# First expert stage of a two-layer kernel: four token buffers, expert numbers read ahead, the output bias added by VectorE, and the next layer's first row begun inside the stage

## The chip, the cores and the metric

The kernel is one program on one core of a Trainium2 chip. The metric is the device time of one launch in microseconds (us). One execution of the kernel before was also profiled, with every engine's instructions recorded; its span runs from the first recorded instruction to the last.

## The reference, cut to what matters

Two layers, each of which adds to a residual the product of an attention and a gated mixture of experts, over 8 rows of 512 tokens with 128 channels:

```python
x = L0_attn_x                                   # (8, 512, 128), float32
xn = _layernorm(x)
s = _L0_attn_ref(xn, ...)                       # 16 heads, top-8 sparse attention, memory keys
g = _silu(_L0_ffn_ref(xn, ...))                 # 8 experts, top 2
x = x + s * g
xn = _layernorm(x)
s = _L1_attn_ref(xn, ...)                       # attention over channels
g = _silu(_L1_ffn_ref(xn, ...))                 # 8 experts, top 2, limited capacity
x = x + s * g
```

The change is in the first mixture of experts, which for each token and each of its two experts `e` computes

```python
h1 = X @ W1[e] + b1[e];  h3 = X @ W3[e] + b3[e]      # 128 -> 256 each
h = silu(h1 * h3)
y = h @ W2[e] + b2[e]                                # 256 -> 128
```

and mixes the two results with the gate's weights. The last product with `Wf` is folded into `W2` and `b2` beforehand.

## The kernel before, in words

The five engines run their own programs and meet only at semaphores. Layer 0's attention is done row by row (`row(b)` on every engine): row 0, then the expert stage for all tokens, then rows 1 to 7; layer 1 follows. While row 0 runs, GpSimd scatters the normalised tokens in DRAM (`x0_slots`) into tiles of 128 that each belong to one expert; `tile_e` holds the expert's number of each of the 72 tiles. The expert stage then takes 18 groups (q) of 4 tiles, in 36 duos (d) of 2 tiles, so that q = d // 2. One duo goes through this chain:

- SyncE loads a group of tokens into one of two buffers `xg0[q % 2]`; TensorE turns it into the bank `tr` (`turned0`); ScalarE and VectorE split it into a high and a low part (`high0`, `low0`), again two buffers.
- TensorE: `up0(d)`, 6 matmuls of 512 columns, the weights chosen by a register that holds the expert's number.
- VectorE: `hidden0(d)`, two adds of the expert's bias out of the banks, also chosen by number. GpSimd: the product of the two halves, into `hu0`. ScalarE: `tanh0`. VectorE: `silu0`, into `hh0`.
- TensorE: `hh_turned0(d)` into the bank `sa`; ScalarE: `turned0(d)` copies it out; TensorE: `down0(d)`, into one of the two banks `mbs[q % 2]`.
- When a group's two duos are done, ScalarE copies the bank to `y0_sb[q % 2]` (`y0_out`), GpSimd adds the output bias of each tile's expert in four adds (`y0_bias`), and SyncE stores the group to `y0_slots` (`store_y0`).

On TensorE the order is written out by hand: iteration d does `up0(d)`, at even d `turned0(d // 2 + 1)`, then `hh_turned0(d - 2)` and `down0(d - 3)`. An expert's number is read from `tile_e` by `value_load`, an instruction of the engine's sequencer, directly ahead of the instruction that uses it, once per tile on TensorE (line 1799), VectorE (line 1365) and GpSimd (line 698). SyncE's queue is in order too: the load of group q, then the store of group q - 4, then, early on, a load of 256 KB of `x` for later.

After the stage TensorE waits for the last `y0_out`, turns row 1's tokens (`x_turned(1)`), ScalarE and VectorE split them (`x_highs`, `x_lows`), and row 1 begins with `keys(1, 0, 0)`, three matmuls from `mt_hl`, which GpSimd splits (`split_m`) after its last `y0_bias`. `scores` needs those keys copied out by ScalarE and VectorE and a piece from GpSimd (`next_g`).

Of the kernel before, what the change touches and what calls it, by code (L numbers as in the profile page):

```python
# [30 lines left out]
P = 128  # L31
# [45 lines left out]
def build(nc, x, Wq, Wk, Wv, pre, post, mem_k, mem_v, Wo, bo, W1, b1, W3, b3, W2, b2, Wg, bg, Wf, bf,  # L77
          norm_w, norm_b, qkv_w, qkv_b, proj_w, proj_b, Wr, V1, c1, V2, c2, out, x0_slots, y0_slots, x_slots, y_slots):
    with ExitStack() as ctx:
# [148 lines left out]
        xg0 = [y0_pick[:, i, :, :] for i in range(2)]  # L228
# [92 lines left out]
        xg0_loaded = [sem("xg0_loaded0"), sem("xg0_loaded1")]  # L321
# [11 lines left out]
        y0_copied = sem("y0_copied")  # L333
# [165 lines left out]
        def _(sp):  # L499
# [65 lines left out]
            for q in range(GROUPS0):  # L565
                if q >= 2:
                    sp.wait_ge(xg0_turned, q - 1)
                sp.dma_start(xg0[q % 2], x0_slots[q * T:(q + 1) * T].rearrange("(s p) c -> p s c", p=P)
                             ).then_inc(xg0_loaded[q % 2], 16)
                if q >= 4:  # L570
                    store_y0(q - 4)
                if q == 2:
                    sp.wait_ge(su_pe, SU_BIASES)
                    sp.wait_ge(raw_read, 1)
                if 2 <= q < B + 2:
                    sp.dma_start(x1_all[:, q - 2, :].rearrange("p (t c) -> p t c", c=C),
                                 x[q - 2].rearrange("(t p) c -> p t c", p=P)).then_inc(x1_in, 16)
            for q in range(GROUPS0 - 4, GROUPS0):
                store_y0(q)
# [59 lines left out]
        def _(pool):  # L639
# [54 lines left out]

            def y0_bias(q):
                pool.wait_ge(y0_copied, q + 1)
                for j in range(NT):
                    e = pool.value_load(tile_e[0:1, NT * q + j:NT * q + j + 1], min_val=0, max_val=E0 - 1)
                    y = y0_sb[q % 2][:, j * C:(j + 1) * C]
                    ins = pool.tensor_tensor(y, y, b2f_b[:, bass.ds(e, 1), :].rearrange("p o c -> p (o c)"), ALU.add)  # L700
                ins.then_inc(y0_ready, 1)
# [172 lines left out]
            for d in range(DUOS0):  # L874
# [44 lines left out]
        def _(act):  # L919
# [80 lines left out]

            def y0_out(q):
                act.wait_ge(y0_ps, 2 * q + 2)
                if q >= 2:
                    act.wait_ge(y0_stored[q % 2], 16 * (q // 2))
# [208 lines left out]
        def _(dve):  # L1213
# [987 lines left out]
```

## Time and profile before

| | us |
|---|---|
| median of 3 runs | 1522.11 |
| lowest and highest | 1516.35, 1522.14 |
| the profiled execution's time | 1525.78 |
| its span | 1524.0 |
| TensorE busy | 1395.9 (92%) |
| VectorE busy | 1102.7 (72%) |
| GpSimd busy | 888.6 (58%) |
| ScalarE busy | 809.9 (53%) |

The profile calls TensorE PE (its weight loads PEld), VectorE DVE, ScalarE ACT, GpSimd POOL and SyncE SP; a q behind the name is the engine's sequencer or queue. Buffer numbers are left out of names (`y_pick` is `y0_pick`, `x_slots` also `x0_slots`, `h` is `h1`, `sc` the five score banks). Busy time is a share of the whole span, over stages with different limits. The expert stage lies between about 243 and 389 us. The profiled execution took 1.8 us more than its span.

### The profile page before, as it was taken

The page shows a single profiled execution, that of the slowest core. Times are in us where ns is not written, and L with a number is a line of the kernel's source. Part 1 is how long each engine was busy: PE and PEld are TensorE (multiplying, and loading weights), DVE is VectorE, ACT ScalarE, POOL GpSimd, SP SyncE. Part 2 cuts the span into 40 slices and gives each one's busy share as a digit, 9 for nine tenths or more (in the row PEclk, how much of TensorE's full clock was granted, in tenths as well). Part 3 has the DMA queues.
Part 4 walks back from the last instruction along what each step waited for, and adds up shares of the span by engine and source line. Part 5 has one row for each costly group of instructions (what it writes and reads, how often), then busy time and mean ns, then how long its engine had stood idle before and what let it go on. Part 6 is the DMA issues. An engine that isn't in the chain of part 4 may idle for free.

```text
span 1524.0 us, 32740 instructions
## 1 busy us (share of the span) xinstructions
PE 1395.9 (92%) x10049; PEld 1201.6 (79%) x10049; DVE 1102.7 (72%) x3639; ACT 809.9 (53%) x1737; POOL 888.6 (58%) x1766
## 2 busy tenths in 40 slices
PE   5999998888799899999999999999999999899964
PEld 5558887777688789888988988898898889788842
DVE  7727775566587678878878887887887778654765
ACT  4546663444455556656665656666566566532321
POOL 5247773667666745655574565557456576723552
PEclk9999999999899999999999999999999999999997
DMA  7025001322500000000000000000000000012221
GB/s 242 15 94 187 22 23 54 105 77 64 159 15 9 17 11 9 8 13 16 8 17 12 9 10 12 15 9 17 12 10 7 6 24 9 10 43 69 75 78 41
DMA packets 70108, 62.27 MB, mean 41 GB/s; under 512 B 10808, under 2 KB 58019, under 8 KB 69938
## 3 DMA queue, kind: packets, MB, share of 16 engines
q1 hardware_dynamic: 61746, 44.96, 9.8%
q0 software_dynamic: 8192, 15.23, 3.4%
q8 instruction: 84, 1.38, 0.4%
q14 instruction: 86, 0.70, 0.2%
HBM read 32.88 MB, written 25.17 MB: 38 GB/s over the span
## 4 chain that ended last, share of the span: by engine, by line
PE 63%; DVE 13%; issue 8%; POOL 7%; ACT 3%; POOLq 2%; DMA 2%; DVEq 1%; SPq 0%; ACTq 0%
PE sa L1863 15%; PE sc L1841 11%; PE mb L1870 11%; PE tr L1852 7%; PE sc L1707 4%; DVE kept L1401 3%; DVE top L1391 3%; POOL attn L797 2%; PE mb L2077 2%; PE sc L1843 2%; PE sc L1802 2%; POOL x_slots L766 1%; PE sa L1907 1%; PE tr L1712 1%; PE sc L2065 1%
## 5 line engine op out<-in xcount | busy, mean ns | idle before, releaser
L797 POOL TENSOR_SCALAR attn<-kept,rden 128x128 f32<-128x128 f32 (+3 forms) x512 | 286.4, 559 | 368.5 <-DVE rden L1405 314.4
L1863 PE MATMUL sa<-wv,attnT 128*128 128x128 f32 x2560 | 383.5, 281 | 16.3 <-ACT wv L1010 15.2
L1391 DVE MAX8 top<-sc 128x8 f32<-128x144 f32 (+3 forms) x512 | 263.2, 514 | 174.0 <-PE sc L1843 172.1
L1841 PE MATMUL sc<-k_hl,x_hl 128*128 128x272 f32 (+3 forms) x1920 | 374.2, 315 | 3.1 <-issue 3.1
L1034 ACT ACTIVATE attnT<-tr 128x128 f32<-128x128 f32 (+3 forms) x512 | 223.7, 437 | 267.5 <-PE tr L1852 257.3
L1863 PEld LDWEIGHTS sa<-wv,attnT 128*128 128x128 f32 x2560 | 327.8, 193 | 44.7 <-ACT wv L1010 44.5
L1028 ACT ACTIVATE ex<-sc,nmax 128x144 f32<-128x144 f32 (+3 forms) x512 | 276.6, 540 | 94.3 <-DVE nmax L1393 86.2
L1841 PEld LDWEIGHTS sc<-k_hl,x_hl 128*128 128x128 f32 x1920 | 284.8, 192 | 22.7 <-issue 12.3
L1401 DVE SCALAR_TENSOR_TENSOR kept<-sc,top,ex 128x144 f32<-128x144 f32 (+3 forms) x512 | 289.4, 565 | 1.1 <-issue 1.1
L1852 PE MATMUL tr<-ident,attn 128*128 128x128 f32 x1280 | 230.0, 278 | 25.6 <-POOL attn L797 23.3
L1852 PEld LDWEIGHTS tr<-ident,attn 128*128 128x128 f32 x1280 | 139.6, 143 | 34.9 <-POOL attn L797 31.8
L802 POOL TENSOR_SCALAR attn_mem<-kept,rden 128x16 f32<-128x16 f32 x512 | 144.2, 282 | 0.0
L1870 PE MATMUL mb<-n_all,xnT 128*128 128x128 f32 x1024 | 142.1, 282 | 0.0
L1870 PEld LDWEIGHTS mb<-n_all,xnT 128*128 128x128 f32 x1024 | 126.2, 194 | 0.0
L1843 PE MATMUL sc<-causal,ident_h 128*128 128x128 bf16 x512 | 118.7, 232 | 0.0
L1870 PE MATMUL mb<-x_hl,w_hl 128*128 128x512 f32 x336 | 108.9, 433 | 5.1 <-POOL w_hl L710 3.7
L1010 ACT ACTIVATE k_hl<-mb 128x512 fp32r<-128x512 f32 x128 | 76.5, 597 | 62.9 <-PE mb L1870 62.7
L1383 DVE TENSOR_TENSOR k_hl<-mb,k_hl 128x512 fp32r<-128x512 f32 x128 | 88.5, 692 | 12.0 <-ACT k_hl L1010 11.3
L1405 DVE RECIPROCAL rden<-den 128x1 f32<-128x1 f32 x512 | 83.9, 164 | 17.8
L691 POOL DMA_INDIRECT x_slots<-arena,take x64 | 66.7, 1042 | 43.6 <-DVE take L1335 30.1
L1393 DVE TENSOR_SCALAR nmax<-top 128x1 f32<-128x1 f32 x512 | 78.7, 154 | 17.6
L1010 ACT ACTIVATE wv<-mb 128x512 f32<-128x512 f32 x128 | 76.1, 595 | 5.4 <-PE mb L1870 5.4
(330 smaller groups left out, 1993.0 us busy)
## 6 DMA issues: line engine op xcount, KB each, us to landing
x_slots<-sg SPq DMA_DIRECT2D x1, 4608.0 KB, 17.1
y_pick<-x_slots SPq DMA_DIRECT2D x18, 256.0 KB, 3.1
y_slots<-wv SPq DMA_DIRECT2D x18, 256.0 KB, 2.4
x_slots<-sg SPq DMA_DIRECT2D x1, 2560.0 KB, 17.3
fb<-L_ffn_b SPq DMA_DIRECT2D x2, 1024.0 KB, 10.4
arena<-L_attn_x SPq DMA_DIRECT2D x8, 256.0 KB, 3.2
fb<-L_ffn_W SPq DMA_DIRECT2D x8, 256.0 KB, 6.1
fb<-x_slots SPq DMA_DIRECT2D x16, 128.0 KB
```

The lines of the kernel that those rows point to most:

```text
L797: pool.tensor_scalar(dst, src[:, NM:NM + P * (t + 1)], rden[:, t:t + 1], 1.0, ALU.mult, ALU.mult).then_inc(attn_ready.sem, 1)
L802: pool.tensor_scalar(attn_mem[:, t, 2 * (it % NIT) + head // NT, :], src[:, 0:NM], rden[:, t:t + 1], 1.0, ALU.mult, ALU.mult).then_inc(mem ...
L1010: return act.activation(dst, mb[:, :], ACT.Copy)
L1028: act.activation(keep_slot(ex, u), src, ACT.Exp, bias=nmax[:, t:t + 1]).then_inc(exp_done.sem, 1)
L1034: act.activation(turn_slot(attnT, u), tr[:, 0:P * (t + 1)], ACT.Copy).then_inc(attnT_ready.sem, 1)
L1391: dve.max(top8[:, t, :], src).then_inc(top_done.sem, 1)
L1401: dve.scalar_tensor_tensor(out=keep_slot(kept, u), in0=src, scalar=top8[:, t, 7:8], in1=keep_slot(ex, u), op0=ALU.is_ge, op1=ALU.mult, acc ...
L1841: pe.matmul(dst[:, lo:hi], x_hl[:, a, t * P:(t + 1) * P], k_hl[:, m, k, lo:hi], start=(i == 0), stop=(i == 2 and hi < w), skip_group_check ...
L1843: pe.matmul(dst[:, w - P:w], ident_h[:, :], causal[:, :], start=False, stop=True, skip_group_check=True).then_inc(sc_ready.sem, 1)
L1852: ins = pe.transpose(tr[:, j * P:(j + 1) * P], src[:, j * P:(j + 1) * P], ident[:, :])
L1863: ins = pe.matmul(sa[:, t * C:(t + 1) * C], src[:, j * P:(j + 1) * P], wv[:, j, k, :], start=False, stop=False, skip_group_check=True)
L1870: ins = pe.matmul(mb[:, at:at + width], lhsT, rhs, start=start, stop=stop)
```

## The change

What it does, part by part:

- Groups of tokens are loaded into four buffers in place of two; the two new ones lie in `attn`, which row 0 has done with by then. SyncE's loop now loads group q when group q - 4 has been turned, and stores group q - 7 behind it.
- TensorE and VectorE read the experts' numbers of duo d + 1 right behind the instructions of duo d (`load_experts`), and keep them in registers.
- `y0_out` on ScalarE and `y0_bias` on GpSimd are gone. VectorE adds the bias itself, out of the bank into `y0_sb`, four adds of 128 columns for a group, in iterations 4, 6, ... 38 of its loop, with the registers of `hidden0`. TensorE, which fills the bank again, now waits for that (`y0_ready`).
- `x_turned(1)`, `x_highs(1)` and `x_lows(1)` stand inside the stage's last iterations. The first keys of row 1 are computed from `mt_all`, as in row 0, and not from the halves that `split_m` makes; TensorE starts them when group 16 has its bias, and the scores when group 17 has it.

```diff
-        xg0 = [y0_pick[:, i, :, :] for i in range(2)]
+        xg0 = [y0_pick[:, i, :, :] for i in range(2)] + [attn[:, i * T:(i + 1) * T].rearrange("p (s c) -> p s c", c=C) for i in range(2)]
...
             for q in range(GROUPS0):
-                if q >= 2:
-                    sp.wait_ge(xg0_turned, q - 1)
-                sp.dma_start(xg0[q % 2], x0_slots[q * T:(q + 1) * T].rearrange("(s p) c -> p s c", p=P)
-                             ).then_inc(xg0_loaded[q % 2], 16)
+                if q == 2:
+                    sp.wait_ge(tr_ready.sem, tr_ready.at(1, 0))
                 if q >= 4:
-                    store_y0(q - 4)
-                if q == 2:
+                    sp.wait_ge(xg0_turned, q - 3)
+                sp.dma_start(xg0[q % 4], x0_slots[q * T:(q + 1) * T].rearrange("(s p) c -> p s c", p=P)
+                             ).then_inc(xg0_loaded[q % 4], 16)
+                if q >= 7:
+                    store_y0(q - 7)
+                if q == 4:
                     sp.wait_ge(su_pe, SU_BIASES)
                     sp.wait_ge(raw_read, 1)
...
                 pool.tensor_tensor(hu0[d % 2].rearrange("p (j n) -> p j n", j=2), hb0[d % 2][:, :, 0:HID0],
                                    hb0[d % 2][:, :, HID0:2 * HID0], ALU.mult).then_inc(hu0_ready, 1)
-                if d % 2 and q >= 2:
-                    y0_bias(q - 2)
-            for q in (GROUPS0 - 2, GROUPS0 - 1):
-                y0_bias(q)
-
             pool.wait_ge(up0_ps, DUOS0)
+            next_g(0, 0)
+
             split_m(0, 0)
             split_m(0, 1)
-            next_g(0, 0)
...
-                if d >= 4 and d % 2 == 0:
-                    y0_out(d // 2 - 2)
-            x_turned(1)
-            x_highs(1)
+                if d == DUOS0:
+                    x_turned(1)
+                    x_highs(1)
             row(1, rest)
...
+            def y0_bias(q):
+                dve.wait_ge(y0_ps, 2 * q + 2)
+                if q >= 2:
+                    dve.wait_ge(y0_stored[q % 2], 16 * (q // 2))
+                for j, e in enumerate(experts_of.pop(2 * q) + experts_of.pop(2 * q + 1)):
+                    ins = dve.tensor_tensor(y0_sb[q % 2][:, j * C:(j + 1) * C], mbs[q % 2][:, j * C:(j + 1) * C],
+                                            b2f_b[:, bass.ds(e, 1), :].rearrange("p o c -> p (o c)"), ALU.add)
+                ins.then_inc(y0_ready, 1)
+
+            load_experts(0)
             low0(0)
-            for d in range(DUOS0 + 1):
+            for d in range(DUOS0 + 3):
                 if d < DUOS0:
                     hidden0(d)
-                if d:
+                if d + 1 < DUOS0:
+                    load_experts(d + 1)
+                if 1 <= d <= DUOS0:
                     silu0(d - 1)
                 if d % 2 == 0 and d // 2 + 1 < GROUPS0:
                     low0(d // 2 + 1)
+                if d == DUOS0:
+                    x_lows(1)
+                if d >= 4 and d % 2 == 0:
+                    y0_bias(d // 2 - 2)
...
                 if d % 2 == 0 and q >= 2:
-                    pe.wait_ge(y0_copied, q - 1)
+                    pe.wait_ge(y0_ready, q - 1)
...
             def keys(b, it, k, guard):
-                if b == 0:
+                if b == 0 or (b == 1 and it == 0):
...
                 guard = keys(b, 0, 0, guard)
+                if b == 1:
+                    pe.wait_ge(y0_ready, GROUPS0)
...
+                if d == DUOS0:
+                    x_turned(1, (x0T_low, GROUPS0))
                 if d >= 3:
                     down0(d - 3)
 
-            pe.wait_ge(y0_copied, GROUPS0)
-            pe.wait_ge(hh0T_ready, DUOS0)
-            x_turned(1, None)
+            pe.wait_ge(y0_ready, GROUPS0 - 1)
```

How the instructions stand, at three places. A row is a line of the kernel, the operation, output and inputs; a wait in brackets comes ahead of it; ISA is register arithmetic of the sequencer.

TensorE in iteration 2 of the stage, before: each tile's number (`tile_e`) is read ahead of that tile's three matmuls (`w13_hl` are the weights), and the wait for VectorE (`hb0_ready`) stands ahead of the first reading.

```order
L1799 TENSOR_LOAD tile_e [waits hb0_ready,x0T_low]
L1799 ISA x2
L1802 ISA
L1802 MATMUL sc<-w13_hl,k_hl 128x512 x2
L1802 ISA
L1802 MATMUL sc<-w13_hl,k_hl 128x512
L1799 TENSOR_LOAD tile_e
```

The same place after, from the first matmul of the second tile on to the next duo's first (`hh` is the turned hidden layer):

```order
L1808 MATMUL sc<-w13_hl,k_hl 128x512 x2
L1808 ISA
L1808 MATMUL sc<-w13_hl,k_hl 128x512
L1795 TENSOR_LOAD tile_e
L1795 ISA x2
L1795 TENSOR_LOAD tile_e
L1795 ISA x2
L1713 MATMUL tr<-ident,attn 128x128 [waits x0T_low,xg0_loaded2]
L1713 MATMUL tr<-ident,attn 128x128 x3
L1713 MATMUL sa<-ident,hh 128x128 [waits hh0_ready]
L1713 MATMUL sa<-ident,hh 128x128 x3
L1808 ISA [waits hb0_ready,x0T_low]
```

Both readings have moved behind the duo's matmuls and ahead of the turns, for the duo that follows; the number of readings is the same.

VectorE between two duos, before, at an even iteration (`hh<-hh,ht` is `silu0`, `k_hl<-tr` is `low0`, `hu<-sc` is the next `hidden0`):

```order
L1372 SCALAR_TENSOR_TENSOR hh<-hh,ht 128x512 [waits th0_ready]
L1358 TENSOR_TENSOR k_hl<-tr,k_hl 128x512 [waits x0T_high]
L1365 TENSOR_LOAD tile_e [waits hu0_ready,up0_ps]
L1365 ISA x2
L1366 ISA
L1366 TENSOR_TENSOR hu<-sc,fb 128x512
```

And after, at iteration 4, where the four adds (`wv<-mb`, `wv` being `y0_sb`) come in:

```order
L1358 SCALAR_TENSOR_TENSOR hh<-hh,ht 128x512 [waits th0_ready]
L1340 TENSOR_TENSOR k_hl<-tr,k_hl 128x512 [waits x0T_high]
L1539 ISA [waits y0_ps]
L1539 TENSOR_TENSOR wv<-mb,fb 128x128
L1539 ISA
L1539 TENSOR_TENSOR wv<-mb,fb 128x128
...
L1352 ISA [waits hu0_ready,up0_ps]
L1352 TENSOR_TENSOR hu<-sc,fb 128x512
```

The reading no longer stands between the wait for TensorE (`up0_ps`) and the add; the adds and a wait for TensorE's `down0` (`y0_ps`) stand between `low0` and the next `hidden0`.

ScalarE at the end of the stage, before (`hh<-ht` is `tanh0`, `attnT<-sa` is `turned0`, `wv<-mb` and `wv<-sc` are `y0_out`, `xnT<-tr` and `x_hl<-xnT` are row 1's `x_turned` and `x_highs`):

```order
L993 ACTIVATE hh<-ht 128x512 [waits hh0T_ps,hu0_ready]
L999 ACTIVATE attnT<-sa 128x512 [waits y0_ps,hh0T_ps]
L1005 ACTIVATE wv<-mb 128x512 [waits y0_stored0,y0_ps]
L999 ACTIVATE attnT<-sa 128x512 [waits y0_ps,hh0T_ps]
L1005 ACTIVATE wv<-sc 128x512 [waits y0_stored1,y0_ps]
L1014 ACTIVATE xnT<-tr 128x512 [waits xnT_ps]
L1019 ACTIVATE x_hl<-xnT 128x512 [waits sc_ready,xnT_ready]
```

And after:

```order
L982 ACTIVATE hh<-ht 128x512 [waits hh0T_ps,hu0_ready]
L988 ACTIVATE attnT<-sa 128x512 [waits y0_ps,hh0T_ps]
L997 ACTIVATE xnT<-tr 128x512 [waits xnT_ps]
L1002 ACTIVATE x_hl<-xnT 128x512 [waits sc_ready,xnT_ready]
L988 ACTIVATE attnT<-sa 128x512 [waits y0_ps,hh0T_ps]
L993 ACTIVATE k_hl<-mb 128x512 [waits misc_ready]
```

The two copies of the output are gone, and row 1's two operations stand ahead of the copy for the last duo.

## Rows read from the trace of the kernel before

**Rows 1.** The page's first part: engine, busy us, share, instructions.

```profile
PE 1395.9 (92%) x10049; PEld 1201.6 (79%) x10049; DVE 1102.7 (72%) x3639; ACT 809.9 (53%) x1737; POOL 888.6 (58%) x1766
```

**Rows 2.** Stretches of time: length, busy of PE, PEld, DVE, ACT, POOL; clock; DMA.

```profile
297.00:304.00 7.00, 6.99 (x31) 6.31 (x32) 1.30 (x3) 3.02 (x6) 1.59 (x2) 0.57 0.40 112
...
340.00:372.00 32.00, 30.99 (x189) 24.50 (x189) 22.36 (x34) 14.60 (x28) 24.14 (x30) 1.00 0.22 59
```

**Rows 3.** Waits, 243 to 388 us: who for whom, total us, times, longest.

```profile
PEld sc L1802 <- issue: 16.2, 34, 2.7
...
PE tr L1712 <- DMA y_pick<-x_slots: 7.5, 6, 2.8
```

**Rows 4.** Waits of SyncE's queue in the same stretch.

```profile
SPq L562 <- POOL wv L700: 109.1, 18, 14.2
```

**Rows 5.** TensorE in order of time, first half: start, length, instructions [idle before].

```profile
245.94 1.86 PE L1802 MATMUL sc<-w_hl,x_hl 128*128 x6 [2.57 <-issue]
...
251.69 2.79 PE L1802 MATMUL sc<-w_hl,k_hl 128*128 x6 [1.88 <-DVE k_hl L1358]
...
258.74 1.87 PE L1802 MATMUL sc<-w_hl,x_hl 128*128 x6
...
289.72 1.64 PE L1802 MATMUL sc<-w_hl,x_hl 128*128 x6
...
292.45 1.75 PE L1802 MATMUL sc<-w_hl,k_hl 128*128 x6
297.01 1.12 PE L1712 MATMUL tr<-ident,y_pick 128*128 128x128 f32 x4 [2.81 <-DMA y_pick<-x_slots]
```

**Rows 6.** TensorE in order of time, second half and the start of row 1.

```profile
340.37 1.88 PE L1802 MATMUL sc<-w_hl,k_hl 128*128 x6
...
342.52 0.60 PE L1712 MATMUL sa<-ident,hh 128*128 128x128 f32 x4
342.95 1.06 PE L1822 MATMUL sc<-fb,attnT 128*128 x8
343.76 1.65 PE L1802 MATMUL sc<-w_hl,k_hl 128*128 x6
...
367.01 1.87 PE L1802 MATMUL sc<-w_hl,k_hl 128*128 x6
...
369.97 1.65 PE L1802 MATMUL sc<-w_hl,k_hl 128*128 x6
...
381.16 0.63 PE L1712 MATMUL tr<-ident,xn_xn 128*128 128x128 f32 x4 [1.27 <-ACT wv L1005]
385.47 1.62 PE L1870 MATMUL mb<-x_hl,w_hl 128*128 128x512 f32 x3 [3.68 <-POOL w_hl L710]
388.61 0.89 PE L1841 MATMUL sc<-k_hl,x_hl 128*128 128x144 f32 x3 [1.53 <-issue]
```

**Rows 7.** Instruction groups, 243 to 388 us: busy us, mean ns | idle before.

```profile
L700 POOL TENSOR_TENSOR wv<-wv,fb 128x128 f32<-128x128 f32 x72 | 34.2, 500 | 3.0 <-issue 2.7
...
L879 POOL TENSOR_TENSOR ht<-hu 128x512 f32<-128x512 f32 x18 | 29.4, 1631 | 36.8 <-DVE hu L1366 36.8
L1372 DVE SCALAR_TENSOR_TENSOR hh<-hh,ht 128x512 f32<-128x512 f32 x36 | 28.5, 792 | 7.4 <-ACT hh L993 7.4
...
L1366 DVE TENSOR_TENSOR h<-sc,fb 128x512 f32<-128x512 f32 x36 | 24.9, 692 | 23.6 <-PE sc L1802 13.0 <-issue 9.7
...
L993 ACT ACTIVATE hh<-ht 128x512 f32<-128x512 f32 x36 | 22.6, 628 | 27.6 <-POOL ht L879 27.6
```

**Rows 8.** VectorE's groups over the span, shapes apart: two-input, 128 columns.

```profile
L1610 DVE SCALAR_TENSOR_TENSOR fb<-ex,p_pick,fb 128x128 f32<-128x128 f32 x8 | 2.3, 346 | 0.2
```

**Rows 9.** Line 1799 in 366 to 368 us: ns min/median/max, first and last start.

```profile
L1799 PEldq TENSOR_LOAD <-tile_e x2: 298/400/501, 366.1 to 367.2; - x2
```

**Rows 10.** Line 1810 in 368 to 369 us: the wait behind duo 34's matmuls.

```profile
L1810 PEldq EVENT_SEMAPHORE  x1: 51/51/51, 368.1 to 368.1; - x1
```

**Rows 11.** SyncE's loads of a group, line 568: us from issue to landing.

```profile
DMA to landing us min/median/max: 2.8/3.4/5.1
```

More of the change, by code:

```diff
@@ L320, in build @@
         scattered0 = sem("scattered0")
-        xg0_loaded = [sem("xg0_loaded0"), sem("xg0_loaded1")]
+        xg0_loaded = [sem(f"xg0_loaded{i}") for i in range(4)]
         xg0_turned = sem("xg0_turned")
@@ L565, in _ @@
             for q in range(GROUPS0):
-                if q >= 2:
-                    sp.wait_ge(xg0_turned, q - 1)
-                sp.dma_start(xg0[q % 2], x0_slots[q * T:(q + 1) * T].rearrange("(s p) c -> p s c", p=P)
-                             ).then_inc(xg0_loaded[q % 2], 16)
+                if q == 2:
+                    sp.wait_ge(tr_ready.sem, tr_ready.at(1, 0))
                 if q >= 4:
-                    store_y0(q - 4)
-                if q == 2:
+                    sp.wait_ge(xg0_turned, q - 3)
[4 more added lines that the diff above has]
+                if q == 4:
                     sp.wait_ge(su_pe, SU_BIASES)
                     sp.wait_ge(raw_read, 1)
[L575 to L578, printed above, removed]
+                if 4 <= q < B + 4:
+                    sp.dma_start(x1_all[:, q - 4, :].rearrange("p (t c) -> p t c", c=C),
+                                 x[q - 4].rearrange("(t p) c -> p t c", p=P)).then_inc(x1_in, 16)
+            for q in range(GROUPS0 - 7, GROUPS0):
                 store_y0(q)
@@ L693, in scatter0 @@
                     in_=xn_all[:, r, (n % NT) * C:(n % NT + 1) * C], in_offset=None).then_inc(scattered0, 16)
[L695 to L701, printed above, removed]
             casts = itertools.count(1)
@@ L999, in turned0 @@
                 act.activation(hh0T[d % 2], sa[:, :], ACT.Copy).then_inc(hh0T_ready, 1)
[L1001 to L1004, printed above, removed]
-                act.activation(y0_sb[q % 2], mbs[q % 2], ACT.Copy).then_inc(y0_copied, 1)
             def evacuate(b, it, name, dst):
@@ L1358, in low0, with load_experts @@
                 dve.tensor_tensor(x0T_hl[q % 2][1], tr[:, :], x0T_hl[q % 2][0], ALU.subtract).then_inc(x0T_low, 1)
+            experts_of = {}
+            def load_experts(d):
+                experts_of[d] = [dve.value_load(tile_e[0:1, 2 * d + j:2 * d + j + 1], min_val=0, max_val=E0 - 1) for j in range(2)]
             def hidden0(d):
@@ L1363, in hidden0 @@
                     dve.wait_ge(hu0_ready, d - 1)
-                for j in range(2):
-                    e = dve.value_load(tile_e[0:1, 2 * d + j:2 * d + j + 1], min_val=0, max_val=E0 - 1)
+                for j, e in enumerate(experts_of[d]):
                     ins = dve.tensor_tensor(hb0[d % 2][:, j, :], bank(2 * (d % 2) + j),
@@ L1785, in turned0, with load_experts @@
             def turned0(q):
-                pe.wait_ge(xg0_loaded[q % 2], 16 * (q // 2 + 1))
+                pe.wait_ge(xg0_loaded[q % 4], 16 * (q // 4 + 1))
                 pe.wait_ge(*((x0T_low, q) if q else (memT_ready.sem, memT_ready.at(0, 2))))
-                turn(tr, xg0[q % 2].rearrange("p s c -> p (s c)")).then_inc(xg0_turned, 1)
+                turn(tr, xg0[q % 4].rearrange("p s c -> p (s c)")).then_inc(xg0_turned, 1)
             tile_of = {}
+            def load_experts(d):
+                for i in (2 * d, 2 * d + 1):
+                    tile_of[i] = pe.value_load(tile_e[0:1, i:i + 1], min_val=0, max_val=E0 - 1)
             def up0(d):
                 q = d // 2
+                if d == 0:
+                    load_experts(0)
                 pe.wait_ge(x0T_low, q + 1)
```

7 lines of the change are left out of this document (3 added, 4 removed).

## Prediction

> **What bounds the kernel now.** I read the page's busy shares first: TensorE works for 92% of the span [rows 1], so a change counts where TensorE stands still or works slowly. The table of stretches and the waits of the expert stage show where that is. In the best stretch, 340 to 372 us, TensorE is busy almost throughout at a granted clock of 1.00; from 297 to 304 us the clock is 0.57 of full speed, hardly above the lower level, 1.2 GHz [rows 2]. The stage's waits name two causes: TensorE's weight loads sat 34 times behind its own sequencer ("issue", 16.2 us), and its turns of new tokens waited 7.5 us for a load from DRAM [rows 3]. A third is at the end: the first matmul of row 1 waited 3.68 us for GpSimd [rows 6].
>
> The timeline of TensorE gives the stage's length. The first `up0` starts at 245.94, the fifth at 258.74 [rows 5], the last at 369.97, and row 1's first scores at 388.61 [rows 6]. So the filling of the pipeline takes 12.8 us, the 31 duos between the fifth and the last 111.2 (3.59 each), and the end 18.6. In the best stretch eight duos, 340.37 to 367.01, take 26.6 us, 3.33 each [rows 6]. With nothing late, a duo without a turn of tokens takes 2.73 (289.72 to 292.45) [rows 5]. By the starts from 342.52 to 343.76 a turn of `hh` is 0.43 of that and a `down0` 0.81 [rows 6], which leaves 1.49 for an `up0`. A turn of tokens is four matmuls of the same shape as the turn of `hh` and adds 0.43 every other time: 2.95 on average. I compare those three figures, 3.59, 3.33 and 2.95.
>
> **The filling.** Before, the third `up0` waits 1.88 us for `low0(1)` on VectorE, which stands behind `hidden0(0)` and its two readings of numbers. The readings leave that path. I follow the new one from 245.9, with 1.49 for an `up0` and the means of [rows 7]: the first `up0` ends at 247.4, the second at 249.3; VectorE finishes `hidden0(0)` at 248.8 (two of 0.69), `low0(1)` at 249.5, `hidden0(1)` at 250.9; GpSimd's product 1.63, the tanh 0.63, `silu0` 0.79, the turn of `hh` 0.43 and `down0` 0.81 lead to 255.2. I add 0.9 for hand-overs and a slow clock, so that the fifth `up0` starts at 256.1, not 258.74: **2.6 us**, between 0 (all of it lost again) and 3.5 (no hand-overs).
>
> **The late loads.** 3.59 against 3.33 over 31 duos is 8.0 us. It is waiting for tokens, with the slow clock after the longest such wait: at 297.01 TensorE had been idle for 2.81 us [rows 5], and then came the stretch at 0.57. The cause is SyncE's order: the load of the next group stands behind the store of an older one, and that store waited for GpSimd's adds 18 times, 109.1 us in all [rows 4]. Now a load goes out when the group four earlier has been turned, three groups or some 18 us before its use, against 2.8 to 5.1 us to its landing [rows 11]; the stores come seven groups late, so SyncE waits for none. The eight 256 KB loads of `x` still stand between them, two groups later than before. **8.0 us**, at least 6 (most of the 7.5 of waiting, and nothing for the clock).
>
> **The steady duos.** How far does 3.33 fall towards 2.95? TensorE first. Its two readings now stand behind `up0`. One reading takes 0.3 to 0.5 us, and two, with the issue of three matmuls between them, began 1.1 us apart [rows 9], so two cost 1.0 to 2.2 us of the sequencer. Covered they are only if the sequencer is ahead by then. In duo 34 it stood at the wait behind the last matmul at 368.1 [rows 10], while those matmuls ran until 368.88 (367.01 + 1.87) [rows 6]: 0.8 us ahead, with one reading still within the duo. Without that one it would be up to 1.1 further ahead, 1.9 in all; I cost TensorE's readings at nothing. VectorE's stand behind `hidden0`, whose adds keep VectorE busy for 1.38, and are costed at nothing too; what reaches beyond that delays `silu0`. If only 0.8 were to be had, 0.4 a duo (1.2 less 0.8) would be exposed, and 3.35 would stand where 2.95 was: no gain here. The Trainium skill, Advanced Engine Details and Errata, section Engine Queue Depths, gives TensorE a queue of 64 instructions. By that all twelve instructions of an `up0` fit in it, and the readings are covered; the row only shows that the sequencer gets ahead, not how far it may.
>
> The chain next. Hidden layer, product, tanh and `silu0` take 1.38 + 1.63 + 0.63 + 0.79 = 4.4 us [rows 7], and `hh_turned0` comes two duos after `up0`, 5.9 us at TensorE's best. Before, the two readings (over 1 us) and on GpSimd the four adds of 0.50 stood in that chain as well. So the chain fits, with GpSimd holding nothing but the product; ScalarE loses a copy of 0.6 us per group and is not near a limit.
>
> VectorE is what remains. In a pair of duos it has four adds of `hidden0` (0.69), two `silu0` (0.79), one `low0` of the same size (0.69) and now the four bias adds. The trace has no such add on VectorE; the nearest row is a two-input operation of 128 columns, 2.3 us for eight in a row, 0.29 each [rows 8], so 1.15 in all. The far bound is GpSimd's own time for the same add, 0.50 [rows 7], so 2.0. I take 0.29, since size, inputs and engine are the same. The sum is 2.76 + 1.58 + 0.69 + 1.15 = 6.18 for a pair, 3.09 a duo: above TensorE's 2.95. I forecast 3.09: **31 x (3.33 - 3.09) = 7.4 us**. The far bound gives 3.52 (a loss of 5.9), TensorE's own limit 2.95 (a gain of 11.8).
>
> `silu0` averages 0.79 us where `hidden0`'s adds of the same width average 0.69 [rows 7]; the first reads both inputs from SBUF, the second one of them from PSUM. The Trainium skill, SBUF — State Buffer, section Who interferes with whom, says that a VectorE instruction with two SBUF inputs and a GpSimd instruction that reads SBUF block each other, and that one with a single SBUF input does not contend. The rows agree with it. By that rule the new adds, one input of which is in PSUM, are never held up, and GpSimd's removed ones hold up no `silu0`; with 0.69 for `silu0` VectorE needs 5.98 a pair, 2.99 a duo, and the gain is 10.5 in place of 7.4, the time 1493.6.
>
> **VectorE's new wait.** At an even iteration VectorE now stands at `y0_ps` until `down0(d - 3)` is done; behind it in the queue is `hidden0(d + 1)`, for which the next `up0`s wait. Counted from the end of `up0(d)`, TensorE finishes that `down0` after 0.43 + 0.43 + 0.81 = 1.7 us; VectorE gets there after `hidden0`, `silu0` and `low0`, 1.38 + 0.79 + 0.69 = 2.9. The wait is over 1.2 us before VectorE comes, so it costs nothing while that lead lasts.
>
> **The end.** Before, TensorE waits for the last `y0_out` (1.27), then the turned tokens pass ScalarE and VectorE, and the keys wait 3.68 for GpSimd, which splits `mt_all` after its last adds [rows 6]. After, counted from the end of the last `up0`: hidden layer 1.4, product 3.0, tanh 3.7. ScalarE then copies duo 34 (4.3), the turned tokens (4.9), their high part (5.5) and only then duo 35 (6.2, each 0.6 as the tanh row); `down0(35)` ends at 7.0. VectorE: row 1's low part 6.3, group 16's bias 7.4. The keys take about 0.9 on TensorE (an estimate, between a third and all of an `up0`), ScalarE's copy 0.6, VectorE's 0.7: scores at about 9.7, while group 17's bias is done by 8.6. From the start of the last `up0` that is 1.5 + 9.7 = 11.2 in place of 18.6: **7.4 us**, between 4 and 9, the low end if row 1 then waits for something that its late start hid (the store of group 17, 2.8 to 5.1 us by the landing row, for which GpSimd waits).
>
> **The sum.** 2.6 + 8.0 + 7.4 + 7.4 = 25.4 us. The span goes from 1524.0 to 1498.6; with the 1.8 us around it the profiled execution would take 1500.4. Its own time, 1525.8, is 3.7 above the median of the runs shown; taken off, the forecast is 1496.7 us, 1.7% less than 1522.1.
>
> **The rivals.**
> - *VectorE, or TensorE's readings, keep the duo at 3.33 or more.* For it: VectorE has the least room after the change, and the price of its adds is from another operation. Against it: adds that follow each other overlap, and the 0.8 us lead was measured with a reading in the way. The steady term is then 0 to -5.9, the gain 18.0 to 12.1, the time 1504 to 1510. Chance 0.22.
> - *TensorE becomes the only limit.* 2.95 and the better ends of filling and tail give 3.5 + 8.0 + 11.8 + 9.0 = 32.3, so 1490. For it speaks `silu0`'s 0.1 us. Chance 0.14.
> - *The gain is given back.* VectorE at its far bound and row 1 losing the head start: 2.6 + 8.0 - 5.9 + 0 leaves 4.7, so 1517. Both would have to come. Chance 0.06.
> - *Slower: VectorE's wait closes a loop.* If `down0(d - 3)` is done after VectorE has got to it, each us is lost once per group on the engine that feeds the next `up0`. It takes 1.2 + 25.4 / 18 = 2.6 us of lateness to use up the gain; a whole duo late, about 3.1 a group with no lead left, costs 56 us: about 1553. Against it stands the 1.2 us lead. Chance 0.04.
>
> **How the numbers follow.** The chance of the forecast is 0.54, for 1491 to 1503. Half a percent, 7.6 us, is about what a measurement of this kernel tells from no change. Only the last two rivals are not faster by that, so faster has 0.90, same 0.06, slower 0.04. The range takes in the first two rivals' times, with a little on either side: 1488 to 1510.
>
> **What would show it.** Right: no wait of TensorE for tokens, the clock at 1.00 from the fifth duo on, duos of 3.0 to 3.2, GpSimd idle between products, bias adds of about 0.3 on VectorE, scores 11 us after the start of the last `up0`. Wrong: "issue" ahead of `hh_turned0`, VectorE without a pause while TensorE waits for its `hh` or hidden layers, VectorE idle at `y0_ps`, or in row 1 a new wait of GpSimd for the stores.

## The result, and the profile after

The changed kernel takes 1500.95 us (median of four executions, 1499.43 to 1503.78) where the kernel before takes 1522.12 beside it: a ratio of 0.9864, with a 95% interval of 0.9836 to 0.9893. That is 1.4% faster, by more than the half percent that can be told from no change, and 4.3 us above the forecast of 1496.7, inside its range. The profiled execution took 1501.5 us with a span of 1499.5; the prediction's sum gave 1498.6 for that span. The total came out nearly as summed, its terms did not.

The page's first part, where [rows 1] stood before: TensorE works 12.7 us less at the same share of the span, and GpSimd 35 us less, since its adds are gone.

```profile
PE 1383.2 (92%) x10047; PEld 1194.6 (80%) x10047; DVE 1121.8 (75%) x3711; ACT 802.5 (54%) x1719; POOL 853.5 (57%) x1694
```

Stretches of the expert stage (columns as in [rows 2]). The granted clock is 0.52, near the lower level of 1.2 GHz, at the first `up0`, and 1.00 from the fifth duo on; the stretch at 0.57 of [rows 2] has no successor. VectorE is busy 38.9 of 43 us, TensorE 41.5.

```profile
247.60:250.60 3.00, 2.94 (x8) 2.26 (x9) 0.00 (x0) 0.00 (x0) 0.00 (x0) 0.52 0.12 34
...
256.00:297.00 41.00, 39.72 (x254) 32.88 (x255) 38.79 (x67) 18.55 (x34) 19.14 (x13) 1.00 0.42 117
297.00:340.00 43.00, 41.48 (x274) 34.95 (x273) 38.94 (x77) 19.80 (x34) 20.19 (x14) 1.00 0.27 75
```

The waits of 243 to 372 us. TensorE's wait for a load of tokens ([rows 3], 7.5 us) is gone, and its weight loads' "issue" ahead of `up0` fell from 16.2 us to 3.6. In their place TensorE waits for `silu0`, 5.4 us in 17 pieces.

```profile
POOL ht L872 <- DVE hu L1352: 47.4, 18, 3.2
...
PEld sa L1713 <- DVE hh L1358: 13.3, 21, 1.2
...
POOL k_hl L712 <- DMA y_slots<-wv: 5.6, 1, 5.6
PE sa L1713 <- DVE hh L1358: 5.4, 17, 1.0
PEld sc L1808 <- issue: 3.6, 2, 3.0
```

TensorE in order of time, for [rows 5] and [rows 6]: the first, the fifth and the last `up0`, and row 1's first scores.

```profile
247.66 2.90 PE L1808 MATMUL sc<-w_hl,x_hl 128*128 x6 [2.87 <-DVE x_hl L1340]
...
259.44 0.94 PE L1808 MATMUL sc<-w_hl,x_hl 128*128 x3
...
358.27 1.64 PE L1808 MATMUL sc<-w_hl,k_hl 128*128 x6
...
370.47 0.53 PE L1849 MATMUL sc<-k_hl,x_hl 128*128 128x144 f32 x3 [1.67 <-DVE k_hl L1369]
```

The differences of such starts say where 24.5 us of span went:

```
piece                                        before   after   gain  forecast
span's start to first up0                    245.94  247.66   -1.7    0
first to fifth up0 (filling)                  12.80   11.78    1.0    2.6
fifth to last up0, 31 duos                   111.23   98.83   12.4   15.4 (8.0 + 7.4)
  a duo                                        3.59    3.19           3.09
last up0 to row 1's first scores              18.64   12.20    6.4    7.4
these scores to row 2's turned tokens        137.4   134.8     2.6    0
from there to the end of the span            998.1   994.3     3.8    0
```

(Row 2's turned tokens are counted from the start of ScalarE's copy of them.) The first and the last line are mostly not the change's. In the twelve experiments below, which leave rows 2 to 7 and layer 1 as they are, the last piece lies between 993.9 and 998.3, and the first `up0` starts between 243.35 and 247.94. For the first `up0` the clock shows where most of that arises: from 100 to 120 us of the span it was 1.00 in the four executions that start it by 243.67 (`u1`, `u3`, `p3`, `p5`) and 0.83 to 0.91 in the other ten, before and after included, which start it from 245.64 on; 3.2 of the 4.3 us by which the changed kernel starts it later than `u1` arise between 105 and 120 us. These two pieces differ from one execution to the next by as much as the terms in dispute, so below I compare the pieces between, and use the whole times for the verdicts.

**The new steady state.** The first four pairs of duos behind the filling take 6.21 to 6.75 us. From 285 us on every pair takes 6.36 us and looks like this one (cut from all engines' instructions in order of time):

```profile
320.09 1.29 POOL L872 TENSOR_TENSOR ht<-h 128x512 f32<-128x512 f32 x1 [0.20 <-DVE h L1352]
...
320.59 1.34 DVE L1358 SCALAR_TENSOR_TENSOR hh<-hh,ht 128x512 f32<-128x512 f32 x1 [0.57 <-ACT hh L982]
...
321.85 0.68 DVE L1340 TENSOR_TENSOR x_hl<-tr,x_hl 128x512 fp32r<-128x512 f32 x1
321.99 0.66 PE L1713 MATMUL sa<-ident,hh 128*128 128x128 f32 x4 [0.22 <-DVE hh L1358]
322.45 0.87 DVE L1539 TENSOR_TENSOR wv<-sc,fb 128x128 f32<-128x128 f32 x4
...
323.25 1.27 DVE L1352 TENSOR_TENSOR hu<-sc,fb 128x512 f32<-128x512 f32 x2
323.29 1.64 PE L1808 MATMUL sc<-w_hl,x_hl 128*128 x6
324.44 0.67 DVE L1358 SCALAR_TENSOR_TENSOR hh<-hh,ht 128x512 f32<-128x512 f32 x1
324.60 1.66 POOL L872 TENSOR_TENSOR ht<-hu 128x512 f32<-128x512 f32 x1 [3.21 <-DVE hu L1352]
...
325.08 1.29 DVE L1352 TENSOR_TENSOR h<-sc,fb 128x512 f32<-128x512 f32 x2
...
326.45 1.29 POOL L872 TENSOR_TENSOR ht<-h 128x512 f32<-128x512 f32 x1 [0.20 <-DVE h L1352]
...
326.95 1.34 DVE L1358 SCALAR_TENSOR_TENSOR hh<-hh,ht 128x512 f32<-128x512 f32 x1 [0.58 <-ACT hh L982]
```

The reader is to see three things. TensorE waits 0.22 us for a `silu0` that took 1.34 us instead of 0.67. VectorE was not late with it for want of time: it stood idle for 0.57 us ahead of it. And the two lengths go with which came first: the silu that began 0.50 us after GpSimd's product ended 0.55 us after that product (321.93 against 321.38), while the product that began 0.16 us after a silu took 1.66 us instead of 1.29. So it is in the whole stage: 18 silus began 0.01 to 0.51 us after a product, took 1.83 down to 1.33 us, and each ended 0.55 us after the product did. In the pair above the period can be followed over TensorE: silu's end at 321.93, turn, `down0`, `up0` from 323.29 to 324.93, `hidden0` from 325.08, product from 326.45 to 327.74, silu's end at 328.29, 6.36 us after the first. VectorE is as tight there: from the low part at 321.85 over bias, `hidden0` and silu it has no pause, and the `hidden0` of 325.08 starts as the silu ahead of it ends (325.11), 0.15 us after `up0` has. So the pair does not say which of these two courses comes last.

My theory after this (A): product and silu hold each other up, and the loop through the held-up silu is the pace. Its rivals: VectorE's sum of work is the pace, as the prediction had it (B), or TensorE's own (C). Beside that stands the question which part of the change gave what.

### The profile page after: what moved, and what is told of

Its sections match the earlier page's. It is cut to its first block, busy times and chain, and to the rows that moved or that the text cites. A ratio compares the mean times of both kernels' runs of the same rounds, so it can differ in the third digit from the quotient of the medians.

```text
span 1499.5 us, 32500 instructions
## 1 busy us (share of the span) xinstructions
PE 1383.2 (92%) x10047; PEld 1194.6 (80%) x10047; DVE 1121.8 (75%) x3711; ACT 802.5 (54%) x1719; POOL 853.5 (57%) x1694
## 4 chain that ended last, share of the span: by engine, by line
PE 66%; DVE 14%; POOL 7%; issue 6%; ACT 3%; DVEq 1%; POOLq 1%; DMA 1%; SPq 0%; ACTq 0%
PE sa L1871 15%; PE sc L1849 12%; PE mb L1878 11%; PE tr L1860 7%; PE sc L1708 4%; DVE kept L1387 3%; DVE top L1377 3%; POOL attn L790 2%; PE mb L2087 2%; PE sc L1808 2%; PE sc L1851 2%; POOL x_slots L759 1%; PE sc L2075 1%; PE tr L1713 1%; PE sa L1915 1%
## 5 line engine op out<-in xcount | busy, mean ns | idle before, releaser
L1878 PE MATMUL mb<-x_hl,w_hl 128*128 128x512 f32 x330 | 104.9, 426 | 1.6 <-DVE x_hl L1363 1.6
```

What stands on the lines that cost most here:

```text
L1878: ins = pe.matmul(mb[:, at:at + width], lhsT, rhs, start=start, stop=stop)
```

## The experiments

First each part undone by itself; then the two of the steady duos undone together; then the pace.

**One part undone: the buffers** (`u1`).

```diff
-xg0 = [y0_pick[:, i, :, :] for i in range(2)] + [attn[:, i * T:(i + 1) * T]... for i in range(2)]
+xg0 = [y0_pick[:, i, :, :] for i in range(2)]
...
-    if q >= 7:
-        store_y0(q - 7)
+    if q >= 4:
+        store_y0(q - 4)
```

> The changed kernel with two buffers and SyncE's old order of loads and stores; the rest as changed. Theory A (the late loads were the old pace): TensorE waits for a load at its turns again, a duo goes back from 3.19 us towards 3.59, up to 12.4 us over 31 duos, so about 1513 us; at least 8 us of it by the prediction's own term. Rival B (the bias on VectorE and the numbers read ahead made the pace, the buffers little): a duo of at most 3.3 us, about 1501 to 1505 us.

1501.36 us, ratio 0.9879 (0.9846 to 0.9911); a duo of 3.18 us and no wait of TensorE for tokens. Theory A of this run is refuted. With the bias on VectorE the store's wait ends early enough for two buffers: the loads of groups 5 to 17 land 1.7 to 4.6 us before TensorE turns them, where in the kernel before six of the thirteen landed less than 0.1 us ahead of it.

**The numbers** (`u2`).

```diff
+    e = pe.value_load(tile_e[0:1, i:i + 1], min_val=0, max_val=E0 - 1)
-    e = tile_of[i]
...
-    if d + 1 < DUOS0:
-        load_experts(d + 1)
```

(the same in VectorE's `hidden0`)

> The changed kernel with the experts' numbers read where they are used again, on TensorE's and VectorE's sequencers. Theory A (the prediction's step: the readings hide behind what is queued): nothing, 1499 to 1504 us, a duo of 3.17 to 3.22 us. Rival B (the sequencers stand still for a reading): some 0.1 to 0.2 us more a duo, so 3 to 6 us, 1504 to 1507 us, with idle time of TensorE ahead of the first products.

1499.86 us, 0.9864 (0.9838 to 0.9890). The whole is unchanged, but by two effects that cancel: the filling is longer, 13.01 us, and the duo shorter, 3.14. The stage's waits show the readings, 8.0 us ahead of `up0`, where the changed kernel has none from its fifth duo on; so the readings ahead are hidden from `up0`, as the prediction had it. (A little shows one step further on: in the changed kernel the weight loads of the turn of tokens, which now follows the readings, wait 2.5 us in 7 pieces, TensorE itself 0.2.) But each `hidden0` now comes later, product and silu meet otherwise (silu ahead each time, mean 0.68, the products 1.66), and TensorE's weight loads wait for the silu in only two duos:

```profile
PEld sc L1807 <- issue: 8.0, 24, 0.5
...
PEld sa L1713 <- DVE hh L1361: 0.7, 2, 0.5
```

**The bias on VectorE** (`u3`).

```diff
+    def y0_out(q):
...
+        act.activation(y0_sb[q % 2], mbs[q % 2], ACT.Copy).then_inc(y0_copied, 1)
...
+    if d % 2 and q >= 2:
+        y0_bias(q - 2)
...
-    if d >= 4 and d % 2 == 0:
-        y0_bias(d // 2 - 2)
```

(the copy on ScalarE, GpSimd's adds, and no adds on VectorE)

> The changed kernel with the output copied out of the bank by ScalarE and its bias added by GpSimd, as in the kernel before; four buffers, numbers ahead and the early row 1 stay. Theory A (GpSimd's chain set the pace once the loads are on time, the prediction's term of 7.4 us for the move to VectorE): a duo of about 3.33 us, 31 x 0.15 = 4.5 us more and up to 3 us at the end, so 1505 to 1509 us. Rival B (VectorE is what holds the pace now, and the four additions are its load): a duo of 3.07 us, 31 x 0.12 = 3.7 us less, about 1497 us.

1502.64 us, 0.9882 (0.9848 to 0.9915). Both expectations fail for the duo: it stays at 3.18 us, with GpSimd's adds and without VectorE's. The median is 1.7 us above the changed kernel's, which the two intervals do not tell apart. What the trace shows as lost is in row 1. GpSimd, still adding, comes late to it: its first attention weights start 22.3 us after the last `up0` (16.2 in the changed kernel), after a wait of 5.57 us that the profile calls "issue" here and the landing of the stores in the changed kernel.

```profile
369.09 0.19 POOL L808 COPY put<-take 128x8 uint32<-128x8 uint32 x1
374.84 0.21 POOL L721 CAST k_hl<-g_hl 128x32 fp32r<-128x32 f32 x1 [5.57 <-issue]
375.03 0.37 POOL L799 TENSOR_SCALAR attn<-kept,rden 128x128 f32<-128x128 f32 x1
```

(`u5` below, which has GpSimd's adds too, shows the same: 21.8 us.)

**The early row 1** (`u4`).

```diff
-    if d == DUOS0:
-        x_turned(1, (x0T_low, GROUPS0))
+x_turned(1, None)
-    if b == 0 or (b == 1 and it == 0):
+    if b == 0:
```

(the turn of row 1's tokens comes behind the loop over duos, their high and low parts and its keys' parts too)

> The changed kernel with row 1 begun only after the last down products, its keys from the split G again. Both theories give back what the end of the stage gained: from the last first products to row 1's first scores 18.6 us where it was 12.2, so 6.4 us. Theory A (the extra 2.7 us in row 1 come from TensorE's clock, granted at half at row 1's start in the kernel before and full in the changed one, because TensorE now has no gap there): these come back as well, 1510 us, with a granted clock near 0.5 in the first 6 us of row 1. Rival B (they are row 1's own, from the keys or from the stores being out of the way): 1507 us and a full clock.

1505.33 us, 0.9897 (0.9868 to 0.9927). Scores 16.7 us after the last `up0`, 4.5 more than in the changed kernel and not the 18.6 that both expectations had: the other 1.9 us stay won, with the bias on VectorE (16.3 in `b1`). The clock is at half, the lower level of 1.2 GHz, at row 1's start, after waits of 1.19, 2.14 and 1.53 us on TensorE; in the changed kernel it is 1.00 at that place.

```profile
368.30:372.30 4.00, 1.06 (x5) 0.85 (x6) 1.34 (x5) 1.23 (x2) 0.21 (x1) 0.82 0.57 181
372.30:376.30 4.00, 2.47 (x8) 1.68 (x8) 0.82 (x2) 0.60 (x1) 0.00 (x0) 0.50 0.97 264
376.30:380.30 4.00, 4.00 (x16) 3.26 (x14) 2.20 (x9) 1.47 (x3) 0.00 (x0) 0.50 1.10 339
```

What this half clock costs: from the first scores to GpSimd's first attention weights 5.26 us, here as in the kernel before and in `b1`, the two others with the late row 1, against 4.00 at full clock. That is 1.3 us, half of theory A's 2.7; from those weights to row 2's tokens it is 128.6 here, 130.8 in the changed kernel and 132.1 before, which goes against the clock and is about as wide as executions differ.

**Neither buffers nor bias** (`u5`: the edits of `u1` and `u3` together, of which the core is this).

```diff
-    if q >= 7:
-        store_y0(q - 7)
+    if q >= 4:
+        store_y0(q - 4)
...
+    if d % 2 and q >= 2:
+        y0_bias(q - 2)
```

> The changed kernel with both undone that, undone one at a time, cost the steady duos nothing: two buffers with SyncE's old order, and the output bias by ScalarE and GpSimd; numbers ahead and early row 1 stay. Theory A (either alone cures the same wait: the bias on VectorE ends the store's wait that kept SyncE from the next load, four buffers let the load be asked for before that store): with neither the loads are late again, a duo of 3.5 to 3.6 us, the stage some 11 to 13 us longer than the 98.6 us of either alone, 1512 to 1517 us. Rival B (the early row 1 or the numbers ahead made the pace, not these): a duo near 3.2 us, 1501 to 1504 us.

1506.48 us, 0.9909 (0.9878 to 0.9940). The late loads are back, here over 256 to 356 us:

```profile
PEld tr L1721 <- DMA y_pick<-x_slots: 8.0, 8, 2.1
...
PE tr L1721 <- DMA y_pick<-x_slots: 5.1, 5, 1.6
```

But a duo takes 3.31 us, between the two expectations. Either of the two cures the loads alone (3.18 each); with neither, a duo still loses 0.28 us less than before, out of 0.41, and of the change only the numbers read ahead are left to do that. That is by elimination; no run has them alone. So, it seems, three parts of the change shorten one and the same loop, load, turn, first products, bias, store, next load, and what each gives depends on which others are there.

**The bias on VectorE alone** (`b1`: the kernel before with this part of the change and nothing else).

```diff
-    if d % 2 and q >= 2:
-        y0_bias(q - 2)
...
-    if d >= 4 and d % 2 == 0:
-        y0_out(d // 2 - 2)
...
+    if d >= 4 and d % 2 == 0:
+        y0_bias(d // 2 - 2)
```

(GpSimd's adds, ScalarE's copy, and VectorE's adds in their place)

> The kernel before with one part of the change alone, the output bias added by VectorE out of the bank; two buffers, numbers in place, row 1 after the stage. Theory A: this part alone takes the steady duos to 3.14 to 3.19 us (12 to 14 us less) and frees GpSimd at row 1's start (up to 3 us less), and keeps the late row 1, 1505 to 1509 us. Rival B (the parts are needed together): a duo of 3.33 us or more, 1511 us or later.

1505.22 us, 0.9895 (0.9861 to 0.9929): 15 of the change's 21 us. A duo of 3.15, the filling 13.03, scores 16.3 us after the last `up0`. That is theory A. The other 6 us are about what the early row 1 brings (4.4 by the medians of `u4` and the changed kernel).

**What holds 3.18 us: the product held back** (`p1`).

```diff
-    if d >= 2:
-        pool.wait_ge(hh0_ready, d - 1)
+    if d >= 1:
+        pool.wait_ge(hh0_ready, d)
```

> The changed kernel with GpSimd's product of a duo held back until VectorE's silu of the duo before is done, so that the two, which read both inputs from SBUF, never lie beside each other. Theory A (the pair of duos goes round a loop: silu, low part, bias, hidden, product, tanh, silu; the meeting of product and silu stretches both in it): silu falls from a mean of 1.07 us to 0.70, a pair from 6.36 us to 6.14, where TensorE alone holds it, 3.4 us over the stage, 1497 to 1499 us. Rival B (VectorE's sum of work is the pace, whatever stretches): the product comes later and nothing is won, 6.36 us a pair or more, 1500 to 1506 us.

1494.95 us, 0.9832 (0.9807 to 0.9857). A wait was added, every product starts later, and a duo falls from 3.19 to 2.99 us, 6.1 us in 31 duos. Two groups of 256 to 340 us: silu's mean is 0.69 where it was 1.11 in the same stretch, the product's 1.27 (1.41 and 1.55).

```profile
L1358 DVE SCALAR_TENSOR_TENSOR hh<-hh,ht 128x512 f32<-128x512 f32 x28 | 19.2, 686 | 11.7 <-ACT hh L982 11.7
L872 POOL TENSOR_TENSOR ht<-h 128x512 f32<-128x512 f32 x15 | 19.1, 1272 | 23.0 <-DVE hh L1358 23.0
```

B is refuted: VectorE does the same instructions, bias adds too, in less time, and still waits 11.7 us for the tanh. C is refuted: TensorE does the same work faster. The gain is nearly twice what theory A expected, since I had taken TensorE's own pace from a pair that still held waits (6.14 us).

**VectorE without the bias** (`p2`; the output goes without its bias here).

```diff
-    ins = dve.tensor_tensor(y0_sb[q % 2][:, j * C:(j + 1) * C], mbs[q % 2][:, j * C:(j + 1) * C], ...)
...
+    act.activation(y0_sb[q % 2], mbs[q % 2], ACT.Copy).then_inc(y0_ready, 1)
```

> The changed kernel with the first experts' output copied out of the bank by ScalarE alone and its bias left out, so VectorE is rid of the four additions (0.87 us a pair) and nothing takes them over. Theory A (loop): the loop is 0.87 us shorter than 6.36 and TensorE's own 6.14 us is the pace, 31 x 0.11 = 3.4 us less, 1497 to 1498 us, and not less than that. Rival B (VectorE's sum): the same pace, so the two agree here; rival C (TensorE's pace already, the 0.22 us wait is only where its slack shows): 6.36 us stays, 1500 to 1502 us.

1501.36 us, 0.9862 (0.9832 to 0.9891); a duo of 3.20. That is the number that C had; but C is out by `p1`, where TensorE does the same work at 2.99. B is refuted a second time, from the other side: 0.87 us less work of VectorE in a pair gives nothing. So is the course that I had given to the loop in the expectation, over low part and bias. The groups of 256 to 340 us show the course: silu is still held up (1.09), and VectorE now waits 8.1 us for `up0`, that is, with the additions gone the loop closes over TensorE.

```profile
L1366 DVE SCALAR_TENSOR_TENSOR hh<-hh,ht 128x512 f32<-128x512 f32 x26 | 28.4, 1092 | 5.5 <-issue 5.0 <-ACT hh L982 0.4
...
L1360 DVE TENSOR_TENSOR hu<-sc,fb 128x512 f32<-128x512 f32 x28 | 18.0, 684 | 8.1 <-PE sc L1805 8.1
```

**The order on TensorE** (`p3`).

```diff
+    if d >= 3:
+        down0(d - 3)
     if 2 <= d < DUOS0 + 2:
         hh_turned0(d - 2)
...
-    if d >= 3:
-        down0(d - 3)
```

> The changed kernel with TensorE's down products of a duo written ahead of the turn of the next duo's hidden part, so that silu has 1.06 us more before TensorE waits for it. Theory A (the loop of VectorE, GpSimd and ScalarE is 6.36 us round by itself): TensorE waits elsewhere, 6.3 us a pair, 1499 to 1502 us. Rival C (only the place of one wait on TensorE holds it, the loop has slack): the wait of 0.22 us is gone, 6.14 us a pair, 1497 to 1498 us.

1499.11 us, 0.9861 (0.9837 to 0.9885); 3.14 us a duo. TensorE no longer waits for a silu, and `down0` is out of the loop over TensorE, yet a pair takes 6.27 us with silus of 0.99. That is nearer to theory A than to C. What TensorE loses now shows as "issue", ahead of the turn of tokens, which follows the readings of numbers:

```profile
PEld tr L1713 <- issue: 8.1, 14, 0.7
```

From an `up0` to that turn it is 1.83 us on the mean, 1.48 in `p1` and `p5`. The order of `p3` by itself does not do that: `p6` below has the same order with product and silu parted, and there it is 1.47. The changed kernel has a second course of the same length, all on VectorE from one held-up silu over low part, bias, two `hidden0` and a silu to the next product. `p2` shortens the second and keeps the first, `p3` the first and keeps the second. No run here shortened both without parting product and silu, so that the two hold 6.36 together is argued, not shown.

**The bias in the odd duos** (`p4`).

```diff
-    if d >= 4 and d % 2 == 0:
-        y0_bias(d // 2 - 2)
+    if d >= 5 and d % 2 or d == DUOS0 + 2:
+        y0_bias((d - 4) // 2)
```

> The changed kernel with VectorE's four bias additions moved from the even duos, where they follow the low part, to the odd ones, behind the silu after which VectorE stands idle for 0.57 us a pair; VectorE's work is the same. Theory A (loop): the additions leave the loop and fill the idle time, a pair of 6.14 to 6.2 us, 1497 to 1499 us. Rival B (VectorE's sum of work): 6.36 us a pair, 1500 to 1502 us.

1495.97 us, 0.9830 (0.9803 to 0.9857), but not by the reason given: a duo of 3.19 us, silus of 1.20. Theory A's loop as I had drawn it falls here too: the additions do fill VectorE's idle time, which is then busy for 95.8 of the 98.9 us of the 31 duos (91.3 of 98.8 in the changed kernel), but the silus, held up for longer, take what that frees. From the last `up0` to row 2's tokens it is 144.8 us against 147.0, and the rest cannot be told from the difference of executions.

**Both together** (`p5`: the edits of `p1` and `p4`; `p6`: and that of `p3`).

```diff
-    if d >= 2:
-        pool.wait_ge(hh0_ready, d - 1)
+    if d >= 1:
+        pool.wait_ge(hh0_ready, d)
...
-    if d >= 4 and d % 2 == 0:
-        y0_bias(d // 2 - 2)
+    if d >= 5 and d % 2 or d == DUOS0 + 2:
+        y0_bias((d - 4) // 2)
```

> The changed kernel with GpSimd's product held until the silu before it is done and VectorE's bias additions in the odd duos. Theory A (the two add up: the duos at TensorE's own pace of 2.97 us by the first, some 2 us less behind the stage as the second showed by itself): 1491 to 1493 us. Rival B (the 2 us of the second were that execution's own): as with the first alone, 1494 to 1496 us.

> The same with TensorE's down products written ahead of the turn as well. With the product held back TensorE still waited for a silu in 13 of 31 duos, 3.6 us in all. Theory A: these waits go, a duo of 2.94 to 2.96 us, 1 us less than without, no more than the measurement can tell. Rival B (the turn now comes later and its copy by ScalarE makes the next down products wait): a duo above 3.0 us, 1 to 3 us more.

`p5` takes 1489.04 us, ratio 0.9805 (0.9775 to 0.9835), the best of all and below the changed kernel's interval. A duo takes 2.94 us, and two stretches of it show what limits it now: TensorE is busy 43.00 of 43.00 us, at a clock of 1.00.

```profile
254.00:297.00 43.00, 43.00 (x292) 38.12 (x291) 37.75 (x79) 20.57 (x37) 18.42 (x15) 1.00 0.40 112
297.00:340.00 43.00, 43.00 (x296) 38.57 (x295) 38.49 (x81) 20.98 (x38) 18.70 (x15) 1.00 0.27 74
```

The additions in the odd duos add 0.05 us a duo to what `p1` won, with the last waits for a silu gone from TensorE's weight loads (3.3 us in 256 to 340 us in `p1`, one of 0.3 in `p5`). The busy share alone would not tell the two apart: in `p1` TensorE is busy for 84.00 of 84.00 us in that stretch, at 2.99. `p6` has 2.93 us, the same, and no wait for a silu, as its theory A has it. Its 1497.47 us (0.9832, 0.9802 to 0.9862) come from elsewhere: in the profiled executions its first `up0` starts 4.0 us later than in `p5`, its filling takes 0.9 us more, the stretch from the last `up0` to row 2's tokens 2.3 and the rest 1.5. The first and the last of these are within the spread of executions told above, and the filling has the clock at 0.50 in the first `up0`, against 1.00 in `p5`; what of the 2.3 is the edit's stays open.

## Why the prediction was right, and where its steps were not

**The total.** Right, and partly by luck: 25.4 us were forecast for the span and 24.5 came, of which 2.1 (3.8 less 1.7) lie outside what the change touches. The four terms themselves brought 19.8 (1.0, 12.4 and 6.4); the other 4.7 come from pieces that the prediction had put at nothing.

**The filling, 2.6 us, came out at 1.0.** The path was right, the clock was not. At the clock of 1.00 the same filling took 10.6 us in `u1`, `u3`, `p2` and `p3`, against the 10.2 that I followed (245.9 to 256.1); that is 2.2 us less than before. In the changed kernel's profiled execution it was 0.52 at the first `up0`, which took 2.90 us; in `u1` the same `up0`, behind the same idle time of 2.87 us and the same work before that, took 1.65:

```profile
243.35 1.65 PE L1806 MATMUL sc<-w_hl,x_hl 128*128 x6 [2.87 <-DVE x_hl L1338]
```

Before, the half clock stood at the third `up0` instead (2.79 us at 251.69 [rows 5], a clock of 0.50 there), so the 1.0 compares two fillings that each had one slow `up0`. Why one execution has the higher clock there and another has not stays open. What I missed besides: the first readings stand ahead of the first `low0` and `up0`. From the start of ScalarE's last copy into `memT` to the first `up0` it is 7.40 us with readings ahead and 7.10 without (before, `u2`, `b1`): 0.3 us.

**The late loads and the steady duos, 8.0 + 7.4, came out at 12.4 together.** The step that failed is the split at 3.33 us. It took the best stretch before for a state without late loads, and gave buffers the way to it and bias and readings the way from it. `u1` and `u3` show that each is enough to cure the loads, and that the bias on VectorE gives the steady duo nothing beyond that. The mechanism named for the loads, SyncE's store waiting for GpSimd's adds ahead of the next load, is borne out by `u5`.

**The steady pace, 3.09 forecast and 3.19 measured, was mis-sized by 0.1 us and right for the wrong reason.** "VectorE 6.18 a pair" failed twice. The sum is too large: VectorE's instructions overlap at their ends (four bias adds of 0.275 take 0.87 us, not 1.10), and in `p5` its busy time is 38.5 of 43 us at 2.94 a duo, 5.26 a pair. And VectorE's sum is not the limit: parting silu and product (`p1`) took 0.2 us a duo off with the same instructions. The prediction had the rule for it. The Trainium skill, SBUF — State Buffer, section Who interferes with whom, says that a VectorE instruction with two SBUF inputs and a GpSimd one that reads SBUF exclude each other, and that the one issued first holds the other up for its whole length. The trace agrees: the product was stretched by 0.37 us behind a silu with 0.52 us left to run, and a silu, 0.69 us long by itself, ended 0.55 us after the product, however early it began; so some 0.14 us of the later one run beside the earlier. But I had drawn from it only that the removed adds free `silu0`, and 0.79 for `silu0` from the kernel before; the product stays, its start moves next to the silu, and silu's mean rose to 1.07. The price of the bias adds was right (0.29 forecast, 0.28 measured), TensorE's own limit too (2.95 and 2.94), and the readings of numbers were hidden.

**VectorE's new wait** cost 0.5 us in the whole stage. That rival, and the two that needed VectorE's far bound, are out. The rival of a duo at 3.33 did not come about, TensorE's own limit did only in `p5` and `p6`.

**The end, 7.4 us, came out at 6.4, and 1.3 more behind the first scores.** Scores stood 12.2 us after the last `up0`, not 11.2. The wait for the stores, which I had named for the low end, came: 5.6 us on GpSimd. It cost nothing, since GpSimd then still waited 2.6 us for VectorE. It was a sign that the prediction had named for being wrong, as was, in part, TensorE's wait for `hh` (VectorE did pause, 0.57 us a pair). Not foreseen was that the clock stays at 1.00 at row 1's start, where TensorE's longest wait is now 1.67 us (1.27, 3.68 and 1.53 before [rows 6]): 1.3 us by `u4`. In `u3` and `u5`, with waits of 2.64 and 2.16 us there, it was 0.50 and 0.57 in spite of the early row 1. The remaining 1.3 us of the 2.6 in row 1 stay open.

## What to carry to other kernels

Before adding gains of parts that shorten one loop, ask what each gives when the others are already there: here the bias alone brought 15 of 21 us, and the buffers nothing on top. When VectorE runs an operation with two SBUF inputs and GpSimd reads SBUF too, look at which of them start side by side after the change, not before; ordering them by one more wait can be faster, as it was here, than letting them meet. And take an engine's load from its busy time in a stretch, not from the sum of its instructions' means.

## What was not expected of the hardware

- Product and silu do not share, they take turns: alone 1.28 and 0.69 us, a meeting costs the later one nearly all of the overlap (up to 1.14 us on a silu, 0.47 on a product).
- One more wait made 31 duos 6.1 us shorter (`p1` against the changed kernel: 92.74 and 98.83).
- After the same work and the same 2.87 us of idle time TensorE's granted clock was 0.52 in one execution and 1.00 in another (the changed kernel and `u1`); their fillings took 11.78 and 10.62 us.
